# Gated cross-attention block on one core: scores in row-packed fp32 tiles, computed a second time transposed, and products divided by way of DRAM

## The reference, cut to what matters

```python
# x, ctx: (128, 128, 256); H = 16 heads of D = 16; mask: one (128, 128) for all
def xattn(values, keys, query, mask, Wv, bv, Wk, bk, Wq, bq, Wo, bo):
    v, k, q = values @ Wv + bv, keys @ Wk + bk, query @ Wq + bq     # (N, 128, H, D)
    energy = einsum('nqhd,nkhd->nhqk', q, k)
    energy = where(mask == 0, neg, energy)
    attn = softmax(energy / sqrt(D), axis=-1)
    return einsum('nhqk,nkhd->nqhd', attn, v).reshape(N, 128, 256) @ Wo + bo

x = x + tanh(g_xattn) * xattn(ctx, ctx, layernorm(x), mask, ...)
x = x + tanh(g_ffn) * tanh(layernorm(x) @ W1 @ W2 @ W3 + bias)
```

## Time and profile before

| | |
|---|---|
| median of 3 runs | 1327.19 us (1324.79 to 1328.39) |
| profiled execution, own time | 1329.0 us |
| its span, first to last instruction | 1327.2 us |
| busy share of the span: PE, DVE, ACT, POOL | 94%, 84%, 85%, 82% |
| chain that ended last, by engine | PE 67%, DVE 14%, issue 9%, ACT 6% |
| mean granted clock of TensorE | 0.985 of 2.4 GHz |
| transfers | 138.02 MB, mean 104 GB/s |

### The profile page before, as it was taken

How to read it: one execution, slowest core, us unless ns; L and a number is a source line. 1 busy time by engine, 2 the same in 40 slices (tenths; PEclk the granted TensorE clock), 3 DMA queues, 4 the chain that set the end, 5 groups by cost and what they waited for, 6 DMA issues and landing times.

```text
span 1327.2 us, 46335 instructions
## 1 busy us (share of the span) xinstructions
PE 1242.4 (94%) x12190; PEld 1108.7 (84%) x12190; DVE 1121.4 (84%) x5983; ACT 1125.8 (85%) x4738; POOL 1083.2 (82%) x1590
## 2 busy tenths in 40 slices
PE   2799999999999999999999999999999999999995
PEld 2588888888898888889889888888888888888974
DVE  5689879889888988988888897898888898898882
ACT  1589989989898998989889898998989899899992
POOL 7568878888888888878788887887888888888886
PEclk9999999999999999999999999999999999999997
DMA  3445445454454544545545444455455454454420
GB/s 98 100 84 108 114 103 106 114 110 99 113 121 91 114 114 98 112 111 112 102 106 116 95 115 102 104 116 113 95 114 118 97 111 112 104 108 114 107 57 33
DMA packets 141121, 138.02 MB, mean 104 GB/s; under 512 B 24308, under 2 KB 124536, under 8 KB 140920
## 3 DMA queue, kind: packets, MB, share of 16 engines
q1 hardware_dynamic: 140920, 136.22, 46.8%
HBM read 35.46 MB, written 16.78 MB: 39 GB/s over the span
## 4 chain that ended last, share of the span: by engine, by line
PE 67%; DVE 14%; issue 9%; ACT 6%; POOL 2%; SPq 2%; DMA 1%; DVEq 0%; POOLq 0%; ACTq 0%
PE ps_m L445 16%; PE ps_s L494 13%; PE ps_m L433 12%; PE ps_attT L505 11%; PE ps_a L520 6%; ACT probs L615 4%; PE ps_m L421 4%; DVE negs L743 4%; PE ps_m L430 2%; PE ps_m L442 2%; DVE yT L761 2%; DVE cT L761 1%; DVE den_r L750 1%; DVE wv_raw L755 1%; DVE neg_max L743 1%
## 5 line engine op out<-in xcount | busy, mean ns | idle before, releaser
L615 ACT ACTIVATE probs<-negs,neg_max 128x128 f32<-128x128 f32 x2048 | 795.9, 395 | 81.2 <-DVE neg_max L743 80.9
L345 POOL TENSOR_TENSOR att<-probs,den_r 128x512 f32<-128x512 f32 x512 | 534.5, 1044 | 189.7 <-DVE den_r L750 170.4
L743 DVE CUSTOM_DVE_ANT_0 negs<-ps_s,far 128x128 f32<-128x128 f32 x2048 | 464.7, 283 | 42.6 <-issue 37.5
L615 ACT ACTIVATION_READ_ACCUMULATOR probs<-negs,neg_max 128x1 f32 x2048 | 397.2, 194 | 0.0
L494 PE MATMUL ps_s<-k_blocks,q_parts 128*128 128x512 f32 x1024 | 369.9, 443 | 6.8 <-DMA q_parts<-qT 6.5
L505 PE MATMUL ps_attT<-ident,att 128*128 128x128 f32 x2048 | 308.7, 273 | 2.8 <-POOL att L345 2.7
L505 PEld LDWEIGHTS ps_attT<-ident,att 128*128 128x128 f32 x2048 | 240.3, 141 | 15.8 <-POOL att L345 5.7
L494 PEld LDWEIGHTS ps_s<-k_blocks,q_parts 128*128 128x128 f32 x1024 | 155.7, 192 | 33.4 <-issue 18.6
L743 DVE DVE_READ_ACCUMULATOR2_ANT neg_max<- 128x1 f32 x2048 | 170.3, 83 | 0.0
L755 DVE COPY attT<-ps_attT 128x512 f32<-128x512 f32 x128 | 88.2, 689 | 35.9 <-PE ps_attT L505 35.9
L433 PE MATMUL ps_m<-xT,wq_s 128*128 128x256 f32 x768 | 110.5, 284 | 0.0
(11 more groups left out here) (108 smaller groups left out, 2227.3 us busy)
## 6 DMA issues: line engine op xcount, KB each, us to landing
k_blocks<-kT SPq DMA_DIRECT2D x512, 64.0 KB, 2.4
q_parts<-qT SPq DMA_DIRECT2D x256, 128.0 KB, 2.5
ctx_in<-in_ctx SPq DMA_DIRECT2D x64, 256.0 KB, 2.8
x_in<-in_x SPq DMA_DIRECT2D x64, 256.0 KB, 2.8
k_blocks<-kT SPq DMA_DIRECT2D x512, 32.0 KB, 2.0
out<-y SPq DMA_DIRECT2D x64, 256.0 KB, 2.2
w_s<-in_L_ffn_aux_weight SPq DMA_DIRECT2D x2, 256.0 KB
wk_raw<-in_L_xattn_Wk SPq DMA_DIRECT2D x1, 256.0 KB
```

The source lines that it names most:

```text
L345: nc.gpsimd.tensor_tensor(att[u % 2][:], probs[u % 4][:], den_r[u % 4][:].unsqueeze(2).to_broadcast([P, G, P]), ALU.mult).then_inc(att_rea ...
L615: last = nc.scalar.activation(probs[u % 4][:, j, :], negs[u % 2][:, j, :], ACT.Exp, scale=-1.0, bias=neg_max[u % 2][:, j:j + 1], accum_out ...
L743: last = nc.vector.tensor_tensor_reduce(out=negs[u % 2][:, j, :], in0=ps_s[u % 2][:, j, :], in1=far[:], scale=1.0, scalar=2 * FAR, op0=ALU ...
```

## The change

Pairs stay; a pair is now worked off as two halves, one batch i = 2t + half each, with all 16 heads at once. `k_aug` and `q_aug` hold head dimensions in 32-row groups: 16 rows of the head (the other head's rows are scaled to zero by `parity`), and in the rows of the other head one row that is 1 in k and receives the negative maximum in q. The scalar engine writes them straight from PSUM with a scale column and a bias column, so the transfers of kT and qT, their split into high and low parts and the block form are gone.

For each batch: (1) `scores`: 16 plain fp32 matmuls, K = 32, in four row tiles, into four banks of PSUM (`ps_s`, a single buffer). (2) `keep_energy`: two scalar copies of 1024 elements to SBUF. (3) `mask_energy`: four GpSimd sums of 512. (4) `maxima`: two vector reductions of 1024. (5) `turn_max`: four transposes. (6) `append_max`: a vector sum into `q_aug`. (7) `scores_T`: 16 matmuls as in (1), with k as the stationary side, so the result is transposed and has the maximum taken off. (8) `mask_transposed`: two vector sums of 1024 from PSUM to SBUF. (9) `exponents`: two of 1024. (10) `weigh_values`: 16 matmuls, whose stationary side also has 16 columns of ones, so the sums of weights come with the products. (11) `keep_a`: a scalar copy of 512. The products of a pair are written to DRAM, denominators and products are read back in two shapes, the reciprocals are written and read back repeated over the head dimension, and GpSimd multiplies (`divide_a`). The high part of aT is made by the scalar engine, its low part by GpSimd. The gated sum at the end is one vector operation (`finish`). The bias of o goes into its matmul group. The loop is gone: all 69 steps are written out.

```diff
-        def turns(eng, body):
-            for t in range(BODY):
-                body(Pair(0, t))
-            with eng.Fori(1, NP // BODY - 1) as i:
-                for r in range(BODY):
-                    body(Pair(i, r))
...
+            # SyncE, after load_first and load_later
+            for t in range(LAST + 1):
+                if is_pair(t + 2): load_ctx(t + 2)
+                if is_pair(t - 5): store(t - 5)
...
+                if is_pair(t - 2):
+                    write_a(t - 2)            # waits a_ready, a_landed, den_landed
+                    read_den(t - 2)           # waits sa_landed, recip_ready
+                    read_a(t - 2)             # waits a_norm_ready of t - 3
+                    write_reciprocals(t - 2)  # waits recip_ready
+                    read_wide(t - 2)          # waits r_landed
+                if is_pair(t + 4): load_x(t + 4)
...
+            # GpSimd
+            def mask_energy(i):
+                for j in range(G):
+                    pool.wait_ge(energy_ready, 2 * i + j // HALF + 1)
+                    nc.gpsimd.tensor_tensor(energy[i % 2][:, j], energy[i % 2][:, j], far[:].unsqueeze(1).to_broadcast([P, SLOTS, P]),
+                                            ALU.add).then_inc(masked, 1)
+            def divide_a(p):
+                pool.wait_ge(a_landed, 16 * (p + 1))
+                pool.wait_ge(wide_landed, 16 * (p + 1))
+                wait(pool, aT_high, p)
+                nc.gpsimd.tensor_tensor(a_norm[:], a_rows[:], den_wide[:], ALU.mult).then_inc(a_norm_ready, 1)
+            def low_of_a(p):
+                pool.wait_ge(aT_high, p + 1)
+                wait(pool, o_done, p)
+                nc.gpsimd.tensor_tensor(flat(aT[:, 1]), a_norm[:], flat(aT[:, 0]), ALU.subtract).then_inc(aT_ready, 1)
...
+            for t in range(LAST + 1):
+                if is_pair(t + 2) or is_pair(t - 4):
+                    if is_pair(t + 2): pool.wait_ge(stat1_ready, t + 3)
+                    if is_pair(t - 4): pool.wait_ge(stat2_ready, t - 3)
+                    rstd(t + 2)               # the same nine steps
+                if is_pair(t - 4): normalise_y(t - 4)
+                if is_batch(2 * t): mask_energy(2 * t)
+                if is_pair(t - 3): divide_a(t - 3)
+                if is_pair(t + 2): normalise_x(t + 2)
+                if is_pair(t - 3): low_of_a(t - 3)
+                if is_batch(2 * t + 1): mask_energy(2 * t + 1)
...
+            # TensorE
+            def scores(i):
+                p, n = i // 2, i % 2
+                pe.wait_ge(k_ready, p + 1)
+                pe.wait_ge(q_ready, p + 1)
+                wait(pe, t_masked, 2 * (i - 1))
+                for s in range(SLOTS):
+                    for j in range(G):
+                        rows = slice(j * ROWS, (j + 1) * ROWS)
+                        last = nc.tensor.matmul(ps_s[:, j, s, :], q_aug[p % 2][rows, n, s, :], k_aug[p % 2][rows, n, s, :],
+                                                start=True, stop=True, tile_position=(j * ROWS, 0))
+                last.then_inc(s_done, 1)
+            # scores_T(i): waits q_ready2 i + 1 and energy_ready 2 * (i + 2), swaps the two operands, signals t_done
+            # turn_max(i): waits max_ready 2 * (i + 1); weigh_values(i): waits probs_ready, q_ready2, signals pv_done
...
+            for t in range(LAST + 1):
+                for half in range(2):
+                    i = 2 * t + half
+                    if is_batch(i - 3): weigh_values(i - 3)
+                    if is_batch(i): scores(i)
+                    if half == 0: make_v(t); turn_ctx(t + 1)      # each only if its pair exists
+                    else: make_q(t + 1)
+                    if is_batch(i - 1): turn_max(i - 1)
+                    if half == 0: turn_x(t + 1); turn_y(t - 4)
+                    else: make_o(t - 3)
+                    if is_batch(i - 1): scores_T(i - 1)
+                    if half == 0: make_k(t + 1)
+                    else: make_f(t - 4)
...
+            # scalar engine; spread: four instructions of 128x256, scale and bias columns; keep_energy and exponents: two each
+                    if is_batch(i - 3): keep_a(i - 3)
+                    if half == 1: high_of_a(t - 3)                # waits a_norm_ready
+                    if is_batch(i): keep_energy(i)
+                    if half == 0: keep_v(t); high_of_ctx(t + 1); high_of_x(t + 1); high_of_y(t - 4)
+                    else: spread_q(t + 1)
+                    if is_batch(i - 1): exponents(i - 1)
+                    if half == 0: spread_k(t + 1)
+                    else: tanh(t - 4)
...
+            # vector engine
+            def mask_transposed(i, c):
+                dve.wait_ge(t_done, i + 1)
+                wait(dve, pv_done, i - 1)
+                banks = slice(c * HALF, (c + 1) * HALF)
+                nc.vector.tensor_tensor(probs[i % 2][:, banks].rearrange("p j s q -> p (j s) q"),
+                                        ps_s[:, banks].rearrange("p j s q -> p (j s) q"),
+                                        far_T[:].unsqueeze(1).to_broadcast([P, HALF * SLOTS, P]), ALU.add).then_inc(t_masked, 1)
...
+                    if is_batch(i - 1): maxima(i - 1, 1)
+                    if half == 0: finish(t - 5)
+                    if is_batch(i - 1): append_max(i - 1)
+                    if half == 0: low_of_ctx(t + 1); low_of_x(t + 1); low_of_y(t - 4)
+                    if is_batch(i - 1): mask_transposed(i - 1, 0); mask_transposed(i - 1, 1)
+                    if half == 1: add_residual(t - 3)             # and the moments of y
+                    if half == 1: moments_of_x(t + 3)
+                    if is_batch(i): maxima(i, 0)
+                    if half == 0: reciprocals(t - 2)
```

More of the change, by code:

```diff
@@ L148, in gated_xattn_block @@
[L148 to L152, removed]
-        block = stack.enter_context(nc.Block())
[L160 to L172, removed]
-            def back(self, k):
-                return Pair(self.quot, self.rem - k)
-            def exists(self):
-                return not self.known or 0 <= self.n < NP
@@ L316, in _, with rstd @@
-            for i in range(2):
-                nc.gpsimd.memset(k_blocks[i][:].rearrange("p a b c -> p (a b c)").bitcast(F32), 0.0).then_inc(consts_ready, 1)
-            def rstd_steps(before, first, last):
+            def rstd(run):
                 vp, r, a, b, nm = (ln_t[:, j, :] for j in range(5))
@@ L394, in _, with normalise @@
-            turns(pool, body)
+                for i, step in enumerate(steps):
+                    nc.gpsimd.tensor_tensor(*step).then_inc(ln_step, 1)
+                    pool.wait_ge(ln_step, RSTD * run + i + 1)
+            def normalise(which, dst, src, ready):
+                for i in range(PAIR):
+                    j = which * PAIR + i
+                    nc.gpsimd.tensor_scalar(dst[:, i, :], src[:, i, :], ln_t[:, 1, j:j + 1], ln_t[:, 4, j:j + 1],
+                                            ALU.mult, ALU.add).then_inc(ready, 1)
@@ new lines, in high_of_a, with spread @@
+            def high_of_a(p):
+                high(aT, a_norm[:], a_norm_ready, p + 1, o_done, p, aT_high)
+            def spread(dst, src, scale, bias, ready):
+                for m in range(KT):
+                    for a in range(2):
+                        last = nc.scalar.activation(dst[:, :, 2 * m + a, :], src[:, m * TOK:(m + 1) * TOK].rearrange("p (n q) -> p n q", q=P),
+                                                    ACT.Identity, bias=bias[:, m, a:a + 1], scale=scale[:, a:a + 1])
+                last.then_inc(ready, 1)
@@ L740, in maxima @@
-            def maxima(b, u):
-                for j in range(G):
-                    last = nc.vector.tensor_tensor_reduce(out=negs[u % 2][:, j, :], in0=ps_s[u % 2][:, j, :], in1=far[:], scale=1.0,
-                                                          scalar=2 * FAR, op0=ALU.add, op1=ALU.min, accum_out=neg_max[u % 2][:, j:j + 1])
-                last.then_inc(negs_ready, 1)
-            def reciprocals(b, u):
-                dve.wait_ge(probs_ready, b.times(UNITS, u + 1))
-                nc.vector.reciprocal(den_r[u % 4][:], den[u % 4][:]).then_inc(den_ready, 1)
@@ L770, in low_of_x, with low_of_y, moments @@
             def low_of_x(p):
-                low(xT, ps_m[BANK["xT"]], xT_high, p.times(1, 1), xT_ready)
-            def stats(which, src):
+                low(xT, ps_m[BANK["xT"]][:], xT_high, p + 1, xT_ready)
+            def low_of_y(p):
+                low(yT, ps_m[BANK["yT"]][:], yT_high, p + 1, yT_ready)
+            steps = [0]
+            def moments(which, src, ready):
                 for i in range(PAIR):
@@ L776, in stats @@
                 last.then_inc(dve_step, 1)
-            def moments(which, ready):
+                steps[0] += 1
+                dve.wait_ge(dve_step, steps[0])
                 for i in range(PAIR):
```

1091 lines of the change are left out of this document (541 added, 550 removed).

## The result

The changed kernel takes 1601.24 us (median of 4 runs, 1599.14 to 1606.93) against 1326.53 (1324.79 to 1328.39): 1.2077 times, 95% interval 1.2041 to 1.2114. The forecast was 1560, with 1415 to 1720 as its range. The profiled execution has a span of 1605.1 us.

What follows compares the result with a forecast made beforehand. The prediction took a ring of waits through the engines' in-order queues as the bound, 19.7 + 2 Ts = 23.5 us a pair, above every engine's busy sum. Time = 173 + 59 P gave 1560 us, 80% range 1415 to 1720.

Steps and rivals of the forecast that it cites:

- the ring: Waits across the engines' queues from one low_of_a on GpSimd to the next, forecast at 23.5 us a pair.
- the faster-side rival: GpSimd as the only bound, moments ready when its second mask ends: 18.1 us a pair, 1241 us; chance 0.07.
- Ts: TensorE time of one score pass (scores or scores_T, 32 records), taken as 1.9 us, range 0.9 to 3.6.
- The limit by weight loads: Score passes on TensorE paced by weight loads, 0.088 us a record as for a transpose, 2.8 us a pass.
- a rival with 0.08: TensorE's clock falls at the ring's waits: 1902 us if in every pair, 1730 if in half; chance 0.08.
- the side-by-side rival: Row tiles of the score passes run fully side by side, Ts 0.9: long ring 21.5 us, 1441 us; chance 0.25.
- a sign of being wrong: On TensorE, a granted clock far under 1, listed among the findings that would show the forecast wrong.
- the trip by way of DRAM: Five transfers in a row for products, denominators and reciprocals, 2.2 to 2.8 us each, costed at nothing; up to 8 if uncovered.
- The ends: Time outside the full steps: first tanh at 122 us, four thin steps of about 12, and 3 to finish and store.
- the form of the forecast: Whole kernel's time as 173 + 59 P, giving 1560 us.
- P: Time of one pair in the 59 full steps, forecast at 23.5 us.

Runs made afterwards that it cites:

- e1: Changed kernel with both moments and the residual put ahead of the masked copies in the vector engine's odd half; 1397.15 us, 1.0521 of the kernel before.
- e2: Changed kernel with turn_y, high_of_y and low_of_y of the even half behind scores_T, exponentials and masked copies; 1501.56 us, 1.1324 of the kernel before.
- e9: e7 with spread_k moved on the scalar engine to behind the odd half's keep_energy, ahead of spread_q; 1253.14 us, 0.9441 of the kernel before.
- e4: Changed kernel with scores and scores_T matmuls reordered, head group outside and slot inside, so row tiles are not interleaved; 1878.28 us, 1.4152 of the kernel before.
- e5: e3 with the even batches' turn_max transposes also issued four times; 1547.18 us, 1.167 of the kernel before.
- e8: Changed kernel with finish behind the even half's masked copies in place of ahead of append_max; 1836.46 us, 1.3825 of the kernel before.
- e6: e1 with high_of_a behind the even half's exponentials, ahead of spread_k, and weigh_values also waiting for the previous keep_a; 1373.56 us, 1.0359 of the kernel before.
- e7: e6 with the low part of aT made by the vector engine, ahead of append_max, in place of GpSimd; 1371.6 us, 1.0342 of the kernel before.
- e10: e9 with high_of_a behind the odd half's keep_energy, low_of_a behind append_max, and weigh_values' added wait removed; 1433.78 us, 1.0801 of the kernel before.
- e3: Changed kernel with turn_x issuing its four transposes four times; 1608.63 us, 1.2138 of the kernel before.
- e11: e8 with the store behind read_wide on SyncE in place of ahead of write_a; 1547.72 us, 1.166 of the kernel before.

## Why the prediction was right, point by point

*The bound is a ring of queue orders, no engine's sum.* Right, and shown: e1 and e2 cut the ring at two places by order alone, and gave 204 and 100 us where 182 and 130 were worked out. Both measured gains hold a share of the clock's, which the two sums left out. The busy sums of a pair were 18.7, 18.1, 15.4 and 14.4 in the forecast; the faster-side rival (GpSimd alone as the bound, 18.1 us a pair) is not what this order gives. Nor is e9 that rival, near as its 18.18 is: GpSimd no longer makes the low part of aT there (1.26), still waits 1.06 in the pair shown, and is busy for less than TensorE.

*Terms of the ring, measured against forecast*, from 799.21 to 823.26: make_o 1.97 (1.76); scores_T with its hop 1.24 (2.15); masked copies 2.28 (2.3); residual and moments 2.74 (2.9); rstd, yn and hops 5.06 (4.5); turn_y 1.02 (0.35); scores_T 2.16 (2.15); masked copies to the end of the exponentials 3.35 (3.3); spread_k 1.80 (1.7); keep_a 0.47 (0.5); high_of_a with its hop 0.73 (0.6); low_of_a 1.23 (1.26). Sum 24.05 (23.5).

*The mis-sized terms.* Ts was taken as 1.9; at the full clock it is 1.10 (801.18 to 802.28 on TensorE), near the side-by-side end of 0.9. The Trainium skill's 3.07 for four row tiles ("TensorE: Matmul & The Clock Gate", Part 3) gave 1.2, and the trace agrees: 16 x 0.226 / 1.10 = 3.3; against the same matmuls in file (e4) it is 2.74 / 1.10 = 2.5. The limit by weight loads that I had weighed against it didn't appear in the interleaved order. The clock was only a rival with 0.08: the low level comes in most pairs, for some 3 us of each, not for a whole ring. It adds 0.67 to turn_y and 0.9 to the second scores_T. So the two errors cancelled: the point came out right partly by luck. With Ts 1.1 alone the sum would have been 21.9 and the time 1465, 9% too low. So it was the condition of the side-by-side rival (0.25) that came true, while its 1441 did not: at the full clock e5 takes 22.8 a pair where the rival had 21.5. And the granted clock, 0.884 over the run, is on the way to what the forecast had named as a sign of being wrong.

*rstd was 0.45 longer than priced*: one of its small steps takes 0.65 beside finish. See below.

*Costed at nothing: the trip by way of DRAM.* Right in the changed kernel, where no wait for a_rows or den_wide shows and the reciprocals wait 0.8 us in all; but the cover was thinner than said. I had looked at the transfers behind the previous divide_a and not at finish, store, write_a, read_den, reciprocals. e8 takes that cover away.

*The ends.* First tanh at 136.6 in place of 122; the last pairs 21.1, 13.8, 13.8 and 9.95 us apart. By the form of the forecast the ends are 1605.1 - 59 x 23.89 = 196 against 173. Half of the miss of 45 us in the span is here, half in P.

*Where the expectations behind it failed.* e6 and e7 named GpSimd the bound too early: freeing one wait of an in-order queue moved it to the next call in line (keep_energy behind spread_k and keep_a). e10 aimed at a wait that e9 had already made small, 1.06 us (it is 1.22 in e10), and made high_of_a late, which is in the ring.

## What to carry to other kernels

When queues are in order and buffers single, add up the ring of waits that returns one period later, call by call, and compare it with the busiest engine's sum; here 24.1 against 18.1, and 22% lay in the order of four calls and one subtraction moved to another engine (which by itself, in e7, gave nothing). After each cut read what stands next in the queue that was freed, and the transfers that the moved call holds back on SyncE, since a store in front of a load can cost more than the cut gives. Give moments and other inputs of a slow serial engine the first place behind what releases them; large copies can wait.

## What the runs showed of the hardware

- **Row tiles**: 32 records of fp32, K = 32, 128 columns moving and 128 loaded, take 1.10 us interleaved over four row tiles and 2.74 in file (e4).
- **The clock fell behind idle gaps, but the gap alone doesn't say when.** Idle gaps of 1.29 and 1.76 us with 1.1 us of work between them were followed by 3 us at 0.50 in most pairs. Filling one gap moved the low stretch to the next (e3, same time), filling both ended it in the middle (e5, 3.4% faster with more work). But in e6 TensorE is idle for 1.83 us ahead of turn_max in nearly every pair, and the middle stays at 1.00:

```profile
805.33 0.63 PE L439 MATMUL ps_x<-ident,neg_max 128*128 128x128 f32 x4 [1.83 <-ACT a_den L622]
```

- **GpSimd and a vector operation with two SBUF tensors slow each other.** Wherever finish ran, the GpSimd operation beside it was stretched: an rstd step 0.65 for 0.20 in the changed kernel, the yn normalisation 1.65 for 1.10 in e1, the division 1.75 for 1.30 in e8. finish took 0.74 in the changed kernel, 1.22 in e8 and 1.43 in e11, and in e10 a subtraction took 1.60 for 0.67. The Trainium skill says as much ("GPSIMD Engine Reference", Key points: GpSimd shares its SBUF interfaces with the vector engine and contends with its instructions that have two SBUF inputs). The traces agree. Operations of the vector engine that read one PSUM and one SBUF tensor kept their length beside GpSimd's masks (two masked copies took 2.32 to 2.36 in every trace that I read).

```profile
806.81 1.65 POOL L286 TENSOR_SCALAR yn<-y,ln_t 128x256 f32<-128x256 f32 x2
```

```profile
820.19 1.75 POOL L309 TENSOR_TENSOR a_norm<-a_rows,den_wide 128x512 f32<-128x512 f32 x1
```

The first is of e1, the second of e8 (GpSimd's timeline of each). What the loop's removal does by itself, and what the kernel before would gain from row tiles for its scores, was not tried.
